# Cross-attention context with high and low probabilities in one matmul; output weights split one slot later and first output tile in the second batch's slot

## What is computed

```python
q = (x @ Wq).reshape(B, Sq, H, D)            # H = 16 heads, D = 128
k = (ctx @ Wk).reshape(B, Skv, H, D)         # Skv = 375, ctx rows of 256
v = (ctx @ Wv).reshape(B, Skv, H, D)
q, k = rmsnorm(q, gq), rmsnorm(k, gk)
attn = softmax(einsum('bqhd,bkhd->bhqk', q, k) / sqrt(D), axis=-1)
out = einsum('bhqk,bkhd->bqhd', attn, v).reshape(B, Sq, H * D) @ Wo
x = layernorm(x + out)
```

## Time and profile before

| | |
|---|---|
| time, median of 3 runs | 1049.61 us |
| the three runs | 1045.9, 1049.74, 1049.61 us |
| the profiled execution, its own time | 1046.03 us |
| its span, first to last instruction | 1044.3 us |
| mean granted TensorE clock | 0.999 |
| PE busy, weight loads busy | 98%, 87% of the span |
| DVE, ACT, POOL busy | 69%, 51%, 51% |

### The profile page before, as it was taken

The page is one execution under the profiler, slowest core; times in us unless marked ns, Lnnn a source line. Parts: engine busy times, 40 slices in busy tenths (PEclk is TensorE's granted clock), DMA queues, the critical chain, the costliest instruction groups (busy, mean ns, idle before and its releaser), DMA issues.

```text
span 1044.3 us, 20310 instructions
## 1 busy us (share of the span) xinstructions
PE 1018.9 (98%) x7021; PEld 910.0 (87%) x7021; DVE 722.6 (69%) x1496; ACT 536.6 (51%) x1075; POOL 532.7 (51%) x515
## 2 busy tenths in 40 slices
...
GB/s 279 83 32 2 61 39 153 143 109 157 116 108 114 99 107 111 101 109 116 96 111 115 94 117 109 98 118 136 98 90 1 286 282 386 387 393 399 294 119 113
DMA packets 45273, 153.46 MB, mean 147 GB/s; under 512 B 3768, under 2 KB 4792, under 8 KB 42144
## 3 DMA queue, kind: packets, MB, share of 16 engines
...
...
## 4 chain that ended last, share of the span: by engine, by line
PE 72%; POOL 5%; DVE 4%; issue 3%; ACT 1%; DMA 1%; POOLq 0%; DVEq 0%; ACTq 0%
PE xa_y_ps L86 6%; PE xa_y_ps L88 5%; PE xa_y_ps L87 5%; PE ex_raw_gu_ps L86 4%; PE ex_raw_gu_ps L88 4%; PE ex_raw_gu_ps L87 4%; PE xa_c_ps L1990 4%; PE xa_c_ps L1986 4%; PE xa_c_ps L1985 3%; PE ex_raw_ey_ps L2212 3%; PE xa_turn_ps L2067 3%; PE xa_turn_ps L2023 3%; PE front_k_ps L86 3%; PE front_k_ps L88 3%; PE front_k_ps L87 3%
## 5 line engine op out<-in xcount | busy, mean ns | idle before, releaser
L1300 POOL TENSOR_TENSOR xa_probs<-xa_probs,xa_inv_sum 112x750 f32<-112x750 f32 x63 | 97.9, 1553 | 75.5 <-DVE xa_inv_sum L1640 75.5
L1589 DVE TENSOR_TENSOR xa_kT_lo<-xa_turn_ps,xa_kT_hi 128x750 fp32r<-128x750 f32 x63 | 59.2, 939 | 99.9 <-ACT xa_kT_hi L1388 99.8
L1285 POOL TENSOR_TENSOR k_ms<-k_ss,sum_eps 125x6 f32<-125x6 f32 x63 | 12.6, 200 | 210.8 <-DVE k_ss L1605 210.8
L1985 PE MATMUL xa_c_ps<-xa_probsT_hi,xa_nat 125*128 125x224 f32 x384 | 92.3, 274 | 2.7 <-ACT xa_probsT_hi L1404 2.7
L1986 PE MATMUL xa_c_ps<-xa_probsT_hi,xa_nat 125*128 125x224 f32 x384 | 92.3, 275 | 0.0
L1404 ACT CAST xa_probsT_hi<-xa_turn_ps 125x672 fp32r<-125x672 f32 x62 | 44.6, 720 | 87.2 <-PE xa_turn_ps L2067 87.2
L1288 POOL TENSOR_TENSOR k_inv<-k_ms,neg_half 125x6 f32<-125x6 f32 x63 | 83.5, 1325 | 8.3 <-POOL k_ms L1285 6.7
L1410 ACT ACTIVATE xa_probs<-xa_scores_ps,xa_bias,xa_q_scale 112x375 f32<-112x375 f32 x126 | 82.8, 663 | 5.9 <-DVE xa_bias L1615 4.7
L1985 PEld LDWEIGHTS xa_c_ps<-xa_probsT_hi,xa_nat 125*128 125x128 f32 x384 | 73.6, 192 | 3.5 <-issue 3.1
L1986 PEld LDWEIGHTS xa_c_ps<-xa_probsT_hi,xa_nat 125*128 125x128 f32 x384 | 73.5, 191 | 0.5
L86 PE MATMUL front_k_ps<-land_xa_wk_hi,land_xa_ctx 128*125 128x256 f32 x252 | 71.4, 283 | 1.6 <-DVE front_k_hat L1632 1.2
...
## 6 DMA issues: line engine op xcount, KB each, us to landing
...
```

Source lines behind the costliest of these rows:

```text
L1300: pool.tensor_tensor(probs[0:T, u % 2], probs[0:T, u % 2], inv_sum[0:T, u % 2, :].unsqueeze(2).broadcast_to([T, 2, KV]), ALU.mult).then_in ...
L1589: dve.tensor_tensor(kT_lo[:, :, 0:KV], turn_ps[:, :, 0:KV], kT_hi[:, :, 0:KV].bitcast(F32), ALU.subtract).then_inc(sem["kT_lo_done"], 1)
L1985: pe.matmul(c_view[:, c], nat[0:KT, u % 2, 0, at], probsT_hi[0:KT, :, cols], start=(t == 0), stop=False)
```

## The change

**Context, units 8 to 61.** `probsT_hi` and `probsT_lo` become the two halves of one buffer `probsT`, so that both are one moving operand of 448 columns. A chunk of the context then takes, per tile of rows, one matmul of `nat` high by both halves (448 columns, high and low probabilities beside each other) and one of `nat` low by `probsT_hi` (224). The output of a chunk is 448 columns, a bank: chunk 0 goes to `c_ps`, chunk 1 to the second bank of `turn_ps`. Odd units have 12 matmuls. Even units begin with four that need no low probabilities, then a fifth of 224 columns that does, and have 13 (`context_pairs`). Units 0 to 7, 62 and 63 keep the old form.

**Reading out.** High-times-high plus low-times-high is one half of a bank, high-times-low the other. ACT copies for each chunk the first half to `cT_hi` and the second to `c_second` (four copies of 224 columns for one of 448). DVE makes `c_rest`, first half minus `cT_hi`, after the second copy of the chunk (two of 224). POOL adds `c_rest` and `c_second` to `cT_lo`. Before the next transposes into `turn_ps` TensorE now waits until chunk 1 is read (`second_bank_read`).

**Output tile 0** moves from slots 5 modulo 8 to slots 6 modulo 8.

**Weights.** DVE's `wv_lo` and `wo_lo` move from the end of slots 3 and 4 (modulo 8) to the beginning of slots 4 and 5, behind the context step. POOL's `wo_hi` stays in slot 4 but goes behind `k_ms` and `k_inv`.

```diff
-        probsT_hi, probsT_lo = sb("probsT_hi", [P, 2, KT_N * T], F32R), sb("probsT_lo", [P, 2, KT_N * T], F32R)
+        probsT = sb("probsT", [P, 2, 2, KT_N * T], F32R)
+        probsT_hi, probsT_lo = probsT[:, 0], probsT[:, 1]
+        c_second = sb("c_second", [P, CC, 2, T])
+        c_rest = y_sb[:, 1, 0:CC * 2 * T].rearrange("p (c h t) -> p c h t", c=CC, h=2)
...
-            return None if b == 1 else max(b - 1, 0)
+            return None if b == 0 else b - 1
 
         def tiles_by(u):
 
-            return TILES * (u // B) + max(u % B, 1)
+            return TILES * (u // B) + u % B
...
+        c_pair = [bank[:, 0:4 * T].rearrange("p (l h t) -> p l h t", l=2, h=2) for bank in (c_ps, turn_ps[:, 1])]
...
+                u = s - 3
+                if B <= u < N:
+                    part = slice(u % 2 * T, (u % 2 + 1) * T)
+                    hold(pool, sem["c_rest_done"], i, CC * B, CC * (u - B + 1))
+                    hold(pool, sem["c_second_done"], i, CC * B, CC * (u - B + 1))
+                    pool.tensor_tensor(cT_lo[:, :, :, part], c_rest, c_second[:], ALU.add).then_inc(sem["cT_lo_done"], 1)
...
-                if s % B == 4 and s // B < PAIRS:
-                    split_hi(pool, i, s // B, "wo", wo_raw, wo_hi, "y_ready", TILES, TILES * (s // B))
...
+                if s % B == 4 and s // B < PAIRS:
+                    split_hi(pool, i, s // B, "wo", wo_raw, wo_hi, "y_ready", TILES, TILES * (s // B))
...
+                    for c in range(CC if u >= B else 0):
+                        hold(act, sem["c_ready" if c else "c0_ready"], i, B, u + 1)
+                        act.copy(cT_hi[:, c, :, u % 2 * T:(u % 2 + 1) * T], c_pair[c][:, 0]).then_inc(sem["cT_hi_done"], 1)
+                        hold(act, sem["cT_lo_done"], i, B, u)
+                        act.copy(c_second[:, c], c_pair[c][:, 1]).then_inc(sem["c_second_done"], 1)
...
+                    for c in range(CC if u >= B else 0):
+                        hold(dve, sem["c_second_done"], i, CC * B, CC * (u - B) + c + 1)
+                        hold(dve, sem["cT_lo_done"], i, B, u)
+                        dve.tensor_tensor(c_rest[:, c], c_pair[c][:, 0], cT_hi[:, c, :, part].bitcast(F32),
+                                          ALU.subtract).then_inc(sem["c_rest_done"], 1)
+                if s % B == 4 and s // B < PAIRS:
+                    split_lo(dve, i, s // B, "wv", wv_raw, wv_hi, wv_lo)
+                if s % B == 5 and s // B < PAIRS:
+                    split_lo(dve, i, s // B, "wo", wo_raw, wo_hi, wo_lo)
...
-                if s % B == 3 and s // B < PAIRS:
-                    split_lo(dve, i, s // B, "wv", wv_raw, wv_hi, wv_lo)
-                if s % B == 4 and s // B < PAIRS:
-                    split_lo(dve, i, s // B, "wo", wo_raw, wo_hi, wo_lo)
...
+            def context_pairs(u, i):
+
+                context_loaded(u, i)
+                if u == B:
+                    pe.wait_ge(sem["cT_lo_done"], B)
+                hold(pe, sem["c_rest_done"], i, CC * B, CC * (u - B) - 1)
+                hold(pe, sem["c_second_done"], i, CC * B, CC * (u - B) - 1)
+                hold(pe, sem["probsT_hi_done"], i, B, u + 1)
+                cols = [slice(t * T, (t + 1) * T) for t in range(KT_N)]
+                if u % 2 == 0:
+                    for t in range(KT_N):
+                        pe.matmul(c_pair[0][:, 0], nat_part(u, 1, 0, t), probsT_hi[0:KT, :, cols[t]], start=(t == 0), stop=False)
+                    pe.matmul(c_pair[0][:, 0], nat_part(u, 0, 0, 0), probsT_hi[0:KT, :, cols[0]], start=False, stop=False)
+                    hold(pe, sem["probsT_lo_done"], i, B, u + 1)
+                    pe.matmul(c_pair[0][:, 1], nat_part(u, 0, 0, 0), probsT_lo[0:KT, :, cols[0]], start=False, stop=False)
+                    for t in range(1, KT_N):
+                        mm = pe.matmul(c_pair[0], nat_part(u, 0, 0, t), probsT[0:KT, :, :, cols[t]], start=False, stop=(t == KT_N - 1))
+                    mm.then_inc(sem["c0_ready"], 1)
+                hold(pe, sem["probsT_lo_done"], i, B, u + 1)
+                for c in range(u % 2 == 0, CC):
+                    if c == 1:
+                        squares_taken(i, u + 2, 1)
+                    for t in range(KT_N):
+                        pe.matmul(c_pair[c], nat_part(u, 0, c, t), probsT[0:KT, :, :, cols[t]], start=(t == 0), stop=False)
+                    for t in range(KT_N):
+                        mm = pe.matmul(c_pair[c][:, 0], nat_part(u, 1, c, t), probsT_hi[0:KT, :, cols[t]], start=False,
+                                       stop=(t == KT_N - 1))
+                    mm.then_inc(sem["c_ready" if c else "c0_ready"], 1)
+
+            def second_bank_read(u, i):
+
+                hold(pe, sem["c_rest_done"], i, CC * B, CC * (u - B + 1))
+                hold(pe, sem["c_second_done"], i, CC * B, CC * (u - B + 1))
...
+                    if s - 3 >= B:
+                        second_bank_read(s - 3, i)
```

More of the change, by code:

```diff
@@ L1371, in queries_out, with context_high @@
                 act.activation(q_sq[:, h, :], y_ps[:, 0:HT], ACT.Square).then_inc(sem["q_sq_done"], 1)
+            def context_high(u):
+                act.wait_ge(sem["c_ready"], u + 1)
+                if u % 2 == 0:
+                    act.wait_ge(sem["o_ready"], u // 2)
+                act.copy(cT_hi[:, :, :, u % 2 * T:(u % 2 + 1) * T], c_view).then_inc(sem["cT_hi_done"], CC)
             def slot(s, i):
@@ L1479, in block_x, with context_halves @@
                 act.copy(xb_hi[:], et_ps[:, 0, :]).then_inc(xs["xb_hi_done"], 1)
-            def context_high(u):
-                act.wait_ge(sem["c_ready"], u + 1)
+            def context_halves(u):
                 if u % 2 == 0:
                     act.wait_ge(sem["o_ready"], u // 2)
-                act.copy(cT_hi[:, :, :, u % 2 * T:(u % 2 + 1) * T], c_view).then_inc(sem["cT_hi_done"], 1)
+                for c in range(CC):
+                    act.wait_ge(sem["c_ready" if c else "c0_ready"], u + 1)
+                    act.copy(cT_hi[:, c, :, u % 2 * T:(u % 2 + 1) * T], c_pair[c][:, 0]).then_inc(sem["cT_hi_done"], 1)
+                    act.wait_ge(sem["cT_lo_done"], u)
+                    act.copy(c_second[:, c], c_pair[c][:, 1]).then_inc(sem["c_second_done"], 1)
             def probs_high(u):
@@ L1577, in first_square_sums, with context_low @@
                                       ALU.add).then_inc(sem["qss_done"], 2)
+            def context_low(u):
+                part = slice(u % 2 * T, (u % 2 + 1) * T)
+                dve.wait_ge(sem["cT_hi_done"], CC * (u + 1))
+                dve.tensor_tensor(cT_lo[:, :, :, part], c_view, cT_hi[:, :, :, part].bitcast(F32),
+                                  ALU.subtract).then_inc(sem["cT_lo_done"], 1)
             def slot(s, i):
```

44 lines of the change are left out of this document (28 added, 16 removed).

## The result

| | before | after |
|---|---|---|
| time, median of 5 | 1049.74 us | 1054.07 us |
| the five | 1045.90, 1049.61, 1049.74, 1049.75, 1050.20 | 1051.67, 1053.81, 1054.07, 1055.17, 1055.97 |
| the profiled execution | 1046.03 us | 1053.81 us |

The ratio is 1.0049, 95% interval 1.0025 to 1.0072: the change makes the kernel slower by half a per cent. The forecast was 1046.2 with a range of 1038.5 to 1054. The sign missed, the time is 7.9 us above the forecast, and it lies above the range by 0.07 us. None of its five cases happened.

A forecast was written before the change was run, and what follows sets the result against it. TensorE, busy 98% of the span, was taken as the bound, through the distance between matmul starts. 6.2 - 4.7 - 1.2 + 2.6 + 0.5 = 3.4 us gained, from the median 1049.61 to 1046.2 us; range 1038.5 to 1054.

The forecast's parts named there:

- five cases: Outcomes: sum stands 0.50; fifth matmul free 0.14; slot 5 waits anew 0.14; hand-over always late 0.12; merges save 2.5 ns 0.04.
- Units 8 to 61 are 27 of each: Paired contexts: 27 odd and 27 even units, together saving 27 x 0.229 = 6.2 us on PE.
- an odd unit has the query projection ahead of its context: Odd contexts: 2.4 us of projection ahead, against 1.3 of join in even units, so no wait for low probabilities.
- the cover is k01: Second bank's read-out: k01 covers it for 1.34 us before the transposes load; the read-out needs 1.26.
- what stands ahead of the new steps is short: DVE ahead of the new read-out steps: earlier work is short and ends about when k01 starts.
- Merges: Context matmuls on PE: each merged pair saves 0.0208 us, 0.125 an odd unit, 0.104 an even one, 6.2 in all.
- case 5: Context matmuls: each merge saves only 2.5 ns, 5.5 us less gain, 1051.6 us; chance 0.04.
- The fifth matmul: Even units' context: it waits 0.17 to 0.18 us for the low probabilities, giving back 4.7 us in all.
- The hand-over in the loop: Transposes wait until ACT and DVE have read chunk 1: 0.10 us late in 12 slots, 1.2 us.
- slow pickup of 0.23: PE resumes 0.23 us after a late wait where a register instruction follows, making slots 0 and 4 modulo 8 late.
- takes the room that `wo_hi` leaves: POOL in slot 4: the new addition, below 1.30 us, fits where `wo_hi` stood; no cost was entered.
- Tile and weights: Moved output tile 0 and weight splits: 2.6 us gained over seven pairs, plus 0.5 in the first pair from `wo_hi`.

The follow-up runs named there:

- experiment 2: The kernel before with only output tile 0 and the `wv_lo`, `wo_lo` and `wo_hi` splits moved, context in the old form: median 1042.67 us, ratio 0.9954.

## Why the prediction was wrong, step by step

- **"Units 8 to 61 are 27 of each", every one costed by a slot of the loop.** This is the step that failed. Units 58 to 61 are written out, and for them three sentences of the prediction are false: "an odd unit has the query projection ahead of its context" (not 59 and 61; 4.1 us of waiting and 1.7 of clock, less the 2.6 that the old form waited), "the cover is k01" (not for unit 61; 1.3), "what stands ahead of the new steps is short" (ACT's `up_hi` copies in slot 61, DVE's `first_low` in slot 63; 0.76 and 0.93). These make 6.2 of the 6.4 us. The diff and the slot functions show all of it, and the profile of before had the two waits of 0.9 us that say these contexts have no cover. The stretch is worth 6.4 us; it stood in the sum as a gain of 0.1. Of the 7.9 us between forecast and median this is 6.5, and the late load is 0.5. The forecast took over the 3.6 us by which the median of before lies above its trace; in the trace of after the late ACT stands in their place with 3.8, whether or not the two are the same thing. The remaining 0.9 is within the spread of the executions of after, 1051.7 to 1056.0.
- **Merges**: predicted 0.0208 us a pair, 0.125 an odd slot. Slots 1, 3 and 7 modulo 8 are 0.12 to 0.15 shorter. Right; case 5, with 2.5 ns a merge, would make that 0.015 and is out.
- **The fifth matmul**: predicted 0.17 to 0.18 lost, even slots 0.07 longer; measured 0.08 to 0.09 longer. Right in size, not in shape, which answers the earlier trace rows:

```profile
502.62 0.86 DVE L1661 TENSOR_TENSOR xa_probsT<-xa_turn_ps,xa_probsT 125x672 fp32r<-125x672 f32 x1
...
503.02 0.50 PE L2042 MATMUL xa_c_ps<-xa_probsT,xa_nat 125*128 125x224 f32 x3
503.35 0.27 PE L2043 MATMUL xa_c_ps<-xa_probsT,xa_nat 125*128 125x224 f32 x1
503.54 0.37 PE L2045 MATMUL xa_c_ps<-xa_probsT,xa_nat 125*128 125x224 f32 x1
503.74 0.58 PE L2047 MATMUL xa_c_ps<-xa_probsT,xa_nat 125*128 125x448 f32 x2
```

The fifth matmul (L2045) starts 0.19 behind the fourth instead of 0.11, and the next one 0.20 behind it instead of 0.11. Of the 0.17 lost half is the wait, half a slow restart.
- **The hand-over in the loop**: predicted 1.2 us, in slots 0 and 4; measured nothing. The durations were right, as the earlier trace rows estimated them: ACT copies 347 and 352 to 362 ns (345 taken), DVE 381 to 392 (385), POOL 1.15 us. The transposes follow k01's start after 1.41 to 1.44, as before (1.51 to 1.53 in slots 5, where k01 itself starts slowly, see the next point). What was wrong is the slow pickup of 0.23, read from the earlier trace rows in another place. In slot 40, one of those that the prediction priced, DVE is done 1.21 after k01's start and the load stands at 1.34 all the same:

```profile
534.86 0.29 PE L86 MATMUL front_k_ps<-land_xa_wk_hi,land_xa_ctx 128*125 128x256 f32 x1
...
535.68 0.39 DVE L1620 TENSOR_TENSOR ex_raw_y_sb<-xa_turn_ps,xa_cT_hi 128x224 f32<-128x224 f32 x1 [0.43 <-ACT xa_c_second L1401]
...
536.20 0.13 PEld L2003 LDWEIGHTS xa_turn_ps<-ident,front_q_sq 128*112 128x112 f32 x1
```

- **POOL in slot 4**: "takes the room that `wo_hi` leaves" was false. The addition takes 1.5 there, but POOL also waits 1.3 for `c_rest` before `wq_hi` may start. That is 2.8 in place of the 1.9 of `wo_hi`:

```profile
496.70 1.53 POOL L1283 TENSOR_TENSOR xa_cT_lo<-ex_raw_y_sb,xa_c_second 128x448 fp32r<-128x448 f32 x1 [1.30 <-DVE ex_raw_y_sb L1620]
498.20 1.89 POOL L81 TENSOR_TENSOR land_xa_wq_hi<-land_xa_wq_raw,zero 128x1024 fp32r<-128x1024 f32 x1
...
505.31 0.18 PEld L86 LDWEIGHTS front_k_ps<-land_xa_wk_hi,land_xa_ctx 128*125 128x125 f32 x1 [0.23 <-DVE front_k_hat L1672]
```

k01 waits 0.2 for `k_hat` and restarts 0.1 slow, 6 x 0.3 = 1.8 us that stood at nothing. The prediction named this wait as a sign that it was wrong, without a price.
- **Tile and weights**: predicted 3.1, measured 3.4. In experiment 2 slots 5 and 6 together are 0.42 to 0.44 less than before (0.40), slot 4 of the first pair 0.52 less (0.5), tile 0 at 0.56 behind the transposes, the wait for `kT_hi` in slot 5. All right.

At slot 60 the sum had 3.0 of its 3.4 us, 2.9 from tile and weights and 0.1 from the pairs of units 8 to 57. Measured are 2.9 there: 3.5 from tile and weights (experiment 2 starts slot 60 at 732.63) and 0.5 to 0.6 lost by the pairs. That the two 2.9 agree is luck: in the loop the errors (POOL in slot 4 at nothing, the hand-over too dear, the weights priced low) nearly cancel. The miss is the last four paired units.
